# Post-norm transformer block on one core: the inverse softmax sums and the output weights brought into place by DMAs instead of TensorE transposes

## The chip, the cores and the metric

One core of one Trainium2 chip. The metric is the device time of one execution, in microseconds (us). Its engines work side by side, each through its own list of instructions in order: TensorE (PE in the profile), VectorE (DVE), ScalarE (ACT), GpSimd (POOL), and SyncE (SP), which here only issues DMAs. They wait for one another by semaphores. An engine that waits holds up everything behind the wait in its list, DMAs that it was to issue included.

## The reference, cut to what matters

```python
x = L0_attn_x                                   # (4, 512, 512), float32
x = _layernorm(x + attention(x, w_qkv, b_qkv, w_out, b_out))   # 16 heads of 32, causal softmax
x = _layernorm(x + ffn(x))                      # silu(x Wg^T) * (x Wu^T), then Wd^T; 512 -> 2048 -> 512
# attention: scores = q k^T / sqrt(32) + causal; attn = softmax(scores); out = (attn v) @ w_out.T + b_out
# Wg, Wu, Wd = (int32 weight - 128) * scale per row
```

## The kernel before, in words

Every product in float32 precision is made of two halves, `hi` (rounded, float32r) and `lo` (the rest), so a projection is three matmuls for each of four chunks of the contraction (12 for a tile of 128 x 512).

**Attention** is worked off in 16 **groups** (`GROUPS`): group G = 4b + g has the four heads g of batch b. Each group has 16 **steps** (`STEPS`), and every engine's list is written by the same double loop over groups and steps. In a group:

- step 0 begins on TensorE with the products of probabilities and values that the group before has left (`weighted_values`, L1397), then come scores of query block 2 (step 0), of block 3 (step 3), and of blocks 0 and 1 of the *next* group (step 8). DVE takes each row's maximum from PSUM (`tile_max`, L1054) and ACT the exponentials with their row sums (`exponential`, L846).
- `transpose_task` (L1376) turns the probabilities on TensorE in ten tasks at steps 0, 3, 8, 10, 12 and 15; ACT (even ones, L898) and DVE (odd ones, L497) copy them to `probsT`.
- between them TensorE does **filling** matmuls from a list (`filling`, with how many at each step): values (`v`, L1315), queries and keys (`q`, `k`, L1297) of groups to come, output projections (`o`, L1334) of the batch before. When such a tile is complete, DVE takes it at the next step: for `o` with `outputs` (L1092) and `output_statistics` (L1070, L1072) at the end of the step.
- the output of the group's heads is gathered in `pv_acc`. `inverse_sum` (L1061) makes 1/sum for each query, which lies along partitions, but is wanted along the free dimension. POOL widens it to 32 copies for each head (`widen_inverse`, L729), TensorE transposes that at step 15 (`transpose_inverse`, L1408, four transposes), ACT keeps it in `attT` (`keep_inverse`, L854). In the next group DVE multiplies at step 1 (`normalise`, L1067), ACT rounds at step 2 (`att_hi`, L860), POOL subtracts (`att_lo`, L697). The first products of step 8 wait for `normed`, since they write `pv_acc` again.

Three PSUM banks (`WORK`) go round among filling tiles, transposing tasks, weight tiles and inverse transposes; the order in which they are used (`Banks`) is worked out ahead, and each use waits until the bank's former content is drained.

The 16 weight tiles are transposed on TensorE (`transpose_weights`, L1263), rounded by ACT (`w_hi`, L827) and subtracted by DVE (`w_lo`, L1020). The four of `w_out` come at steps 5 and 13 of groups 3 and 4.

**The next batch's input** comes transposed by DMAs: `turn` (L552) issues 8 transposing DMAs of 16-bit halves, `store_halves` (L556) writes them to DRAM, `load_halves` (L560) reads them back so that POOL can `join` (L718) the halves. From `turn(4)` on the same path brings the first layer norm's output for the feed-forward part.

**SyncE's list** in group G, in this order: load for the scan (a check of the feed-forward weights by ACT, steps 6 and 14; the load waits until the buffer's former content is scanned); `load_halves` in g = 0; `turn` in g = 2; in g = 3 the stores of y1 and the next residual (in the last batch: `load_short(0)`), then `store_halves`. After the groups: scales (L625 to L627), `load_halves(5)`, `load_short(1)`, (2), (3). `load_short(r)` (L580, L583, L586) issues 12 transposing DMAs with a quarter of the gate, up and down weights: 4 each.

**Feed-forward**, batch 0: TensorE does 16 matmuls of gate and up (L1508, L1509) for each of 16 hidden tiles and, one tile later, 8 of down (L1515, L1516). ACT widens the staged weights just ahead (`widen_piece`, L918, L923), makes `silu` (L948) and the product's `hi`; DVE the product and its `lo`. ACT's first silu waits for all three scales:

```python
act.wait_ge(scales_loaded, 48)
...
for i in range(NI):
    gate_out(0, i, gate_acc[first_bank(i)])
```

Of the kernel before, what the change touches and what calls it, by code (L numbers as in the profile page):

```python
# [6 lines left out]
def postln_block_kernel(nc: bass.Bass, x, w_qkv, b_qkv, w_out, b_out, gate_w, gate_scale, up_w, up_scale,  # L7
# [13 lines left out]
    P = 128  # L21
# [32 lines left out]
    def scores_at(G, s):  # L54
        if G == GROUPS - 1:
            return {0: (0, (3,))}.get(s)
        if G == GROUPS - 2 and s == 13:
            return 1, (2,)
        return SCORE_STEPS.get(s)

    def maxima_at(G, s):
        if G == GROUPS - 1:
            return {0: (0, 3, (0, 1)), 1: (0, 3, (2, 3))}.get(s)
        if G == GROUPS - 2 and s == 13:
            return 1, 2, (0, 1, 2, 3)
        return MAX_STEPS.get(s)

    def exponentials_at(G, s):
        if G == GROUPS - 1:
            return {1: (0, 3, (0, 1)), 2: (0, 3, (2, 3))}.get(s)  # L70
        if G == GROUPS - 2 and s > 13:
            return 1, 2, ((0, 1), (2, 3))[s - 14]
# [4 lines left out]
    def tasks_of(hf):  # L77
# [9 lines left out]
    INVERSE_STEP = 15  # L87
    SLOTS = 7
    X_STEPS = [1, 2, 3, 4]
    X_FIRST = [3, 5, 6, 7]  # L90
# [3 lines left out]
        (kind, n) for n in range(2, NG) for kind in "qk"] + [("o", n) for n in range(ND)]  # L94
    NW = len(W_TILES)
    W_STEPS = {(0, 4): 8, (0, 7): 9, (1, 4): 10, (1, 7): 11, (3, 5): 12, (3, 13): 13, (4, 5): 14, (4, 13): 15}
# [7 lines left out]

    W_PLACES = NW - ND

    def w_place(i):
        return i if i < W_PLACES else w_tile("v", i - W_PLACES)

    def w_row(i):  # L110
        kind, n = W_TILES[i]
        return "qkvo".index(kind) * D + n * P
# [9 lines left out]
    def filling(G):  # L122
# [15 lines left out]
        return (before + ahead, AMONG_X) if b < LAST else (before, [4, 4, 0, 4, 0, 4, 2, 0, 2, 0, 2, 0, 2, 0, 0, 0])  # L138
# [59 lines left out]
    for G, (jobs, counts) in enumerate(FILLING):  # L198
        for s in range(STEPS):
# [8 lines left out]
            if s == INVERSE_STEP:  # L208
                banks.whole(("r", G))
# [14 lines left out]
    halves_dram = [None] + [nc.dram_tensor(f"halves{n}", (2 * D, S), U16, kind="Internal").ap() for n in range(1, 2 * B)]  # L224
    x_v = x.rearrange("b (t p) d -> b p t d", p=P)
# [36 lines left out]
    LEVEL_FRONT, LEVEL_INVERSE, LEVEL_PROBS = 40, 16, 24  # L262
# [10 lines left out]
    with ctx:  # L273
# [30 lines left out]
        w_stage = sb("w_stage", [P, W_PLACES, D], F32, front)  # L304
# [13 lines left out]
        wT_hi = sb("wT_hi", [P, ND, NE + D], F32R, att)  # L318
        wT_lo = sb("wT_lo", [P, ND, NE + D], F32R, att)
# [3 lines left out]
        inv_sum = sb("inv_sum", [P, NT, HG], F32, att)  # L323
        sb("level_inverse", [P, LEVEL_INVERSE], F32, att)
        inv_wide = sb("inv_wide", [P, NT, HG, HD], F32, att)
# [71 lines left out]
        xT_done = sem("xT_done")  # L397
        z_loaded = sem("z_loaded")
# [8 lines left out]
        inv_widened = sem("inv_widened")  # L407
# [90 lines left out]

        def y_whole(b):
            return z_tok if isinstance(b, int) and b == 0 else yT_next  # L500
# [8 lines left out]

        block = ctx.enter_context(nc.Block())  # L510

        @block.sync
        def _(sp):

            def load_w(i):
                kind, n = W_TILES[i]
                src = w_out[n * P:(n + 1) * P, :] if kind == "o" else w_qkv[w_row(i):w_row(i) + P, :]
                if i >= W_PLACES:
                    wait_drained(sp, "w", w_place(i))
                sp.dma_start(w_stage[:, w_place(i), :], src).then_inc(w_loaded[i], 16)  # L520
# [15 lines left out]
            for i in range(8, W_PLACES):  # L536
# [24 lines left out]

            def store_y1(b):
# [28 lines left out]
            for i in range(W_PLACES, NW):  # L591
                load_w(i)
# [4 lines left out]
            for G in range(GROUPS):  # L597
                b, g = divmod(G, NG)
                if G in SCAN_GROUPS[1:]:
# [7 lines left out]
                if g == 2:  # L607
                    turn(b + 2)
# [9 lines left out]
                if g == 3:  # L618
                    store_halves(b + 2)

# [46 lines left out]
        def _(pool):  # L667
# [58 lines left out]
            def widen_inverse(G):  # L726

                wait_alone(pool, inv_done, 2 * (G + 1))
                nc.gpsimd.tensor_copy(inv_wide[:, :, :, :], inv_sum[:, :, :].unsqueeze(3).broadcast_to(  # L729
                    (P, NT, HG, HD))).then_inc(inv_widened, 1)  # L730

            def add_bias(b):
# [3 lines left out]
                for t in range(NT):  # L736
                    last = nc.gpsimd.tensor_tensor(residual(b)[:, t, :], residual(b)[:, t, :], bias_o[:, :], ALU.add)  # L737
                last.then_inc(res_ready, 1)
# [24 lines left out]
            for G in range(GROUPS):  # L763
                b, g = divmod(G, NG)
                if g == 2:
                    join(b + 1)
                    if b > 0:
                        next_lo(b + 1, 0)
                        next_lo(b + 1, 1)
                if G > 0:  # L770
                    att_lo(G - 1)
                if g == 2 and b > 0:
                    next_lo(b + 1, 2)
                    next_lo(b + 1, 3)
                if G == GROUPS - 1:
                    apply_norm(LAST - 1, 2)
                    apply_norm(LAST - 1, 3)
                    store_third()
                    choose_path()
                widen_inverse(G)  # L780
                if 1 <= G <= 3 * CHUNKS:
                    shorten(G - 1)
                if g == 2 and b > 0:
                    for t in range(NT if b < LAST else 2):
# [3 lines left out]
            add_bias(LAST)  # L788
# [31 lines left out]
        def _(act):  # L820
# [21 lines left out]

            def exponential(G, qb, j):
# [4 lines left out]

            def keep_inverse(G):
                wait_full(act, "r", G)  # L850
                if G > 0:

                    act.wait_ge(att_ready, G)
                nc.scalar.activation(attT[:, :], bank_of("r", G)[:, :], ACT.Copy).then_inc(drained_of("r", G), 1)  # L854
# [32 lines left out]
            for G in range(GROUPS):  # L887
                b, g = divmod(G, NG)
                for s in range(STEPS):
                    for c in x_at(G, s):  # L890
                        next_hi(b + 1, c)
                    if exponentials_at(G, s):
# [6 lines left out]
                    if s == 2 and G > 0:  # L899
# [3 lines left out]
                    if s == INVERSE_STEP:  # L903
                        keep_inverse(G)
# [739 lines left out]
```

## Time and profile before

| | |
|---|---|
| median of 3 runs | 739.49 us (738.57, 739.49, 745.54) |
| the profiled execution | 738.95 us, span 737.0 us, mean granted TensorE clock 0.993 |
| TensorE matmul busy | 713.1 us (97%) |
| TensorE weight load busy | 552.3 us (75%) |
| DVE / ACT / POOL busy | 390.2 (53%) / 373.7 (51%) / 182.1 us (25%) |
| DMA | 83.35 MB, 113 GB/s on the mean |

The span is from the first to the last instruction; the execution's own time is 1.9 us longer. Busy shares are over the whole span; the attention part ends at about 379 us, and the feed-forward part takes the rest.

### The profile page before, as it was taken

The page shows a single profiled execution, that of the slowest core. Times are in us where ns is not written, and L with a number is a line of the kernel's source. Part 1 is how long each engine was busy: PE and PEld are TensorE (multiplying, and loading weights), DVE is VectorE, ACT ScalarE, POOL GpSimd, SP SyncE. Part 2 cuts the span into 40 slices and gives each one's busy share as a digit, 9 for nine tenths or more (in the row PEclk, how much of TensorE's full clock was granted, in tenths as well). Part 3 has the DMA queues.
Part 4 walks back from the last instruction along what each step waited for, and adds up shares of the span by engine and source line. Part 5 has one row for each costly group of instructions (what it writes and reads, how often), then busy time and mean ns, then how long its engine had stood idle before and what let it go on. Part 6 is the DMA issues. An engine that isn't in the chain of part 4 may idle for free.

```text
span 737.0 us, 11734 instructions
## 1 busy us (share of the span) xinstructions
PE 713.1 (97%) x4368; PEld 552.3 (75%) x4368; DVE 390.2 (53%) x992; ACT 373.7 (51%) x900; POOL 182.1 (25%) x194
## 2 busy tenths in 40 slices
PE   7999899999999999999899999999999999999994
PEld 5776676677777777776578888888888888888883
DVE  4766766566666666677543232453334532544336
ACT  3676676667866776777656555322232222322230
POOL 0011310437122660416655242221020001000004
PEclk9999999999999999999999999999999999999998
DMA  9811553336741567314498964872331003000111
GB/s 305 231 66 29 80 146 119 86 95 119 219 144 58 117 171 223 81 41 115 106 217 162 199 161 143 183 217 85 136 66 57 0 35 136 0 1 1 57 58 59
DMA packets 97207, 83.35 MB, mean 113 GB/s; under 512 B 64128, under 2 KB 73344, under 8 KB 97024
## 3 DMA queue, kind: packets, MB, share of 16 engines
q1 hardware_dynamic: 90624, 62.69, 30.6%
q0 software_dynamic: 6528, 19.93, 12.7%
q8 instruction: 34, 0.56, 0.3%
q14 instruction: 21, 0.17, 0.1%
HBM read 59.53 MB, written 22.02 MB: 111 GB/s over the span
## 4 chain that ended last, share of the span: by engine, by line
PE 90%; POOL 3%; ACT 2%; DVE 2%; DMA 1%; issue 0%; SPq 0%; POOLq 0%; DVEq 0%
PE bank L1508 16%; PE bank L1509 16%; PE bank L1297 12%; PE bank L1376 9%; PE bank L1516 7%; PE bank L1515 7%; PE bank L1315 6%; PE bank L1359 6%; PE bank L1397 5%; PE bank L1334 4%; ACT probs L846 1%; DVE probs L1054 1%; PE bank L1408 1%; PE bank L1263 1%; DMA x_tok<-in_L_attn_x_dram 1%; POOL scan_buf L737 1%
## 5 line engine op out<-in xcount | busy, mean ns | idle before, releaser
L846 ACT ACTIVATE probs<-probs,neg_max 128x128 f32<-128x128 f32 (+3 forms) x256 | 140.4, 552 | 3.9 <-DVE neg_max L1054 3.9
L1054 DVE CUSTOM_DVE_ANT_0 probs<-bank,causal 128x128 f32<-128x128 f32 (+3 forms) x256 | 111.7, 484 | 40.2 <-PE bank L1359 40.0
L1170 DVE SCALAR_TENSOR_TENSOR hid<-bank,u_scale,silu 128x512 f32<-128x512 f32 x64 | 48.1, 751 | 157.5 <-PE bank L1509 156.3
L1508 PE MATMUL bank<-xT_hi,gateT 128*128 128x512 f32 x256 | 99.7, 389 | 0.0
L1509 PE MATMUL bank<-xT_lo,gateT 128*128 128x512 f32 x256 | 99.6, 389 | 0.0
L1508 PE MATMUL bank<-xT_hi,upT 128*128 128x512 f32 x256 | 99.6, 389 | 0.0
L1509 PE MATMUL bank<-xT_lo,upT 128*128 128x512 f32 x256 | 99.6, 389 | 0.0
L1376 PEld LDWEIGHTS bank<-ident,probs 128*128 128x128 f32 x640 | 72.1, 142 | 34.0 <-issue 24.7
L948 ACT ACTIVATE silu<-bank,g_scale 128x512 f32<-128x512 f32 x64 | 44.0, 687 | 102.2 <-PE bank L1509 102.2
L898 ACT ACTIVATE probsT<-bank 128x512 f32<-128x512 f32 x80 | 47.7, 596 | 94.9 <-PE bank L1376 93.2
L954 ACT ACTIVATE hid_hi<-hid 128x512 fp32r<-128x512 f32 x58 | 36.7, 632 | 108.6 <-DVE hid L1170 108.6
L1515 PE MATMUL bank<-downT,hid_hi 128*128 128x512 f32 x232 | 90.2, 389 | 0.0
L1516 PE MATMUL bank<-downT,hid_lo 128*128 128x512 f32 x232 | 90.2, 389 | 0.0
L1376 PE MATMUL bank<-ident,probs 128*128 128x128 f32 x640 | 89.2, 279 | 1.0 <-ACT probs L846 0.5
L497 DVE COPY probsT<-bank 128x512 f32<-128x512 f32 x80 | 54.9, 686 | 26.3 <-PE bank L1376 26.3
L1174 DVE TENSOR_TENSOR hid_lo<-hid,hid_hi 128x512 fp32r<-128x512 f32 x58 | 41.5, 715 | 40.5 <-ACT hid_hi L954 40.5
L1508 PEld LDWEIGHTS bank<-xT_hi,gateT 128*128 128x128 f32 x256 | 48.0, 188 | 10.3 <-DVE hid L1170 0.4
L1509 PEld LDWEIGHTS bank<-xT_lo,upT 128*128 128x128 f32 x256 | 48.1, 188 | 10.0
L1509 PEld LDWEIGHTS bank<-xT_lo,gateT 128*128 128x128 f32 x256 | 48.1, 188 | 10.0
L1508 PEld LDWEIGHTS bank<-xT_hi,upT 128*128 128x128 f32 x256 | 48.0, 188 | 10.0
L1297 PE MATMUL bank<-xT_hi,wT_hi 128*128 128x512 f32 x128 | 54.9, 437 | 0.2
L1359 PE MATMUL bank<-k_sb,q_sb 32*128 32x512 f32 (+3 forms) x512 | 48.1, 467 | 2.6 <-DVE neg_max L1054 2.5
(106 smaller groups left out, 1159.9 us busy)
## 6 DMA issues: line engine op xcount, KB each, us to landing
halves<-x_tok SPq DMA_DIRECT2D x7, 1024.0 KB, 6.2
x_tok<-halves SPq DMA_DIRECT2D x7, 1024.0 KB, 7.9
scan_buf<-in_L_ffn_gate_w_dram SPq DMA_DIRECT2D x4, 1024.0 KB, 6.0
scan_buf<-in_L_ffn_up_w_dram SPq DMA_DIRECT2D x4, 1024.0 KB, 5.5
scan_buf<-in_L_ffn_down_w_dram SPq DMA_DIRECT2D x4, 1024.0 KB, 5.5
w_int<-in_L_ffn_gate_w_dram POOLq DMA_DIRECT2D x16, 256.0 KB, 3.7
w_int<-in_L_ffn_up_w_dram POOLq DMA_DIRECT2D x16, 256.0 KB, 3.2
w_int<-in_L_ffn_down_w_dram POOLq DMA_DIRECT2D x16, 256.0 KB, 3.8
```

The costliest lines, as they stand in the source:

```text
L497: copy(probsT[:, (G * BLOCKS + i) % SLOTS, :], bank_of("t", G, i)[:, :]).then_inc(drained_of("t", G, i), 1)
L846: nc.scalar.activation(probs[qb][:, j, :], probs[qb][:, j, :], ACT.Exp, bias=neg_max[:, qb, j:j + 1], scale=-1.0, accum_out=row_sum[:, qb, ...
L898: evict_task(act, G, i, lambda o, i: nc.scalar.activation(o, i, ACT.Copy))
L1054: nc.vector.tensor_tensor_reduce(out=probs[qb][:, j, :], in0=score[j][:, first:first + w], in1=causal[:, S - w:S], scale=-SCALE, scalar=-F ...
L1170: nc.vector.scalar_tensor_tensor(out=hid[:, i % 2, :], in0=bank[:, :], scalar=u_scale[:, i:i + 1], in1=silu[:, i % 2, :], op0=ALU.mult, op ...
L1297: last = nc.tensor.matmul(acc[:, :], w[:, c, e], xT[:, c, :], start=at == 0, stop=at == MM - 1)
L1359: last = nc.tensor.matmul(score[j][:, first:first + w], q_sb[G % 2][rows, qb * P:(qb + 1) * P], k_sb[G % 2][rows, 0:w], start=True, stop=True)
L1376: last = nc.tensor.transpose(acc[:, m * P:(m + 1) * P], probs[qb][:, j, kb * P:(kb + 1) * P], ident[:, :])
L1508: nc.tensor.matmul(acc[n][:, :], w[:, c, cols], form(xT_hi[:, c, :]), start=c == 0, stop=False)
L1509: last = nc.tensor.matmul(acc[n][:, :], w[:, c, cols], form(xT_lo[:, c, :]), start=False, stop=c == ND - 1)
L1515: nc.tensor.matmul(down_acc[t][:, :], form(hi[:, tok]), w_down[:, i, :], start=i == 0, stop=False)
L1516: return nc.tensor.matmul(down_acc[t][:, :], form(lo[:, tok]), w_down[:, i, :], start=False, stop=i == NI - 1)
```

## The change

- The output weights are no longer transposed on TensorE. SyncE issues 8 transposing DMAs of 16-bit halves in group 0 (`turn_w`), stores them to DRAM and loads them back in group 1; POOL joins them in group 3 (`join_w`), ACT rounds them in group 4 at steps 3, 5, 7, 9 (`w_out_hi`), POOL subtracts (`w_out_lo`).
- The inverse sums: DVE writes them with another layout, transposes them in blocks of 32 x 32 at step 8 (`turn_inverse`), a DMA stores them to DRAM (16 KB) and a second one loads them back, repeated over 32 partitions for each head, into `inv_rows`. SyncE issues both, with a wait for the first ahead of the second; for the last group ACT does, at steps 8 and 10. POOL's widening, the four transposes and ACT's copy go.
- `normalise` moves from step 1 to step 5, `att_hi` from step 2 to step 6; in the last group both stand in step 0.
- `inverse_sum` of the second half moves from step 9 to step 8 (step 5 in the last group).
- In g = 2 SyncE does the inverse's store and load, then the scan load of the following group, and then `turn`.
- POOL instead of DVE subtracts for batch 1 (`next_lo`); the last batch's bias is added in two halves earlier; all four `apply_norm` of batch 2 come in group 14.
- Scores, maxima and exponentials of the last group's query block 2 move from steps 13 to 15 of group 14 into step 0 of group 15; the filling of group 14 ends at step 6.

```diff
     PRODUCT_STEPS = [8, 8, STEPS, STEPS, STEPS, STEPS]
-    INVERSE_STEP = 15
+    TURN = 32
+    STORE_STEP, SPREAD_STEP = 8, 10
-    X_FIRST = [3, 5, 6, 7]
+    X_FIRST = [3, 4, 5, 6]
-    W_STEPS = {(0, 4): 8, (0, 7): 9, (1, 4): 10, (1, 7): 11, (3, 5): 12, (3, 13): 13, (4, 5): 14, (4, 13): 15}
+    W_STEPS = {(0, 4): 8, (0, 7): 9, (1, 4): 10, (1, 7): 11}
+    W_OUT_STEPS = [3, 5, 7, 9]
-        return (before + ahead, AMONG_X) if b < LAST else (before, [4, 4, 0, 4, 0, 4, 2, 0, 2, 0, 2, 0, 2, 0, 0, 0])
+        return (before + ahead, AMONG_X) if b < LAST else (before, AMONG_X[:8] + [0] * (STEPS - 8))
+        def store_inverse(eng, G):
+            eng.wait_ge(inv_turned_done, G + 1)
+            eng.dma_start(inv_dram.rearrange("j (q a r) -> (j q) a r", a=P // TURN, r=TURN).rearrange("c a r -> a c r"),
+                          inv_turned[:, :]).then_inc(inv_stored, 16)
+        def load_inverse(eng, G):
+            eng.wait_ge(inv_stored, 16 * (G + 1))
+            if G > 0:
+                eng.wait_ge(normed, G)
+            eng.dma_start(inv_rows[:, :], inv_dram[:, 0:S].unsqueeze(1).broadcast_to((HG, HD, S))).then_inc(inv_spread, 16)
...
 # SyncE
+            def spread_inverse(G):
+                store_inverse(sp, G)
+                load_inverse(sp, G)
             for G in range(GROUPS):
                 b, g = divmod(G, NG)
-                if G in SCAN_GROUPS[1:]:
+                if G in SCAN_GROUPS[1:] and g != 3:
                     load_scan(SCAN_GROUPS.index(G))
...
                 if g == 2:
+                    spread_inverse(G)
+                    if G + 1 in SCAN_GROUPS:
+                        load_scan(SCAN_GROUPS.index(G + 1))
                     turn(b + 2)
...
                 if g == 3:
                     store_halves(b + 2)
+                if g != 2 and G < GROUPS - 1:
+                    spread_inverse(G)
+                if G == 0:
+                    turn_w()
+                if G == 1:
+                    store_w()
+                    load_w_halves()
...
 # POOL
+                    if b == LAST:
+                        add_bias(LAST, range(QH))
                 if G == GROUPS - 1:
-                    apply_norm(LAST - 1, 2)
-                    apply_norm(LAST - 1, 3)
+                    add_bias(LAST, range(QH, NT))
                     store_third()
                     choose_path()
-                widen_inverse(G)
+                if G == NG - 1:
+                    join_w()
+                if G == NG:
+                    for c in range(ND):
+                        w_out_lo(c)
...
-            add_bias(LAST)
 # ACT
-                    if s == 2 and G > 0:
+                    if s == 6 and 0 < G < GROUPS - 1:
                         att_hi(G - 1)
-                    if s == INVERSE_STEP:
-                        keep_inverse(G)
+                    if s == STORE_STEP and G == GROUPS - 1:
+                        store_inverse(act, G)
+                    if s == SPREAD_STEP and G == GROUPS - 1:
+                        load_inverse(act, G)
 # DVE
+            def turn_inverse(G):
+                if G > 0:
+                    dve.wait_ge(inv_stored, 16 * G)
+                wait_alone(dve, inv_done, 2 * (G + 1))
+                nc.vector.transpose(inv_turned[:, :], inv_sum[:, :, :].rearrange("p j q -> p (j q)")).then_inc(inv_turned_done, 1)
             def normalise(G):
-                wait_drained(dve, "r", G)
+                dve.wait_ge(inv_spread, 16 * (G + 1))
+                if G > 0:
+                    dve.wait_ge(att_ready, G)
                 dve.wait_ge(pv_full, G + 1)
-                nc.vector.tensor_tensor(attT[:, :], pv_acc[:, :], attT[:, :], ALU.mult).then_inc(normed, 1)
+                nc.vector.tensor_tensor(attT[:, :], pv_acc[:, :], inv_rows[:, :], ALU.mult).then_inc(normed, 1)
-                    if s == 1 and G > 0:
+                    if s == 5 and 0 < G < GROUPS - 1:
                         normalise(G - 1)
-                    if s == 9:
+                    if s == (8 if G < GROUPS - 1 else 5):
                         inverse_sum(G, 1)
+                        turn_inverse(G)
 # TensorE
-                    if s == INVERSE_STEP:
-                        last_products = products_at(STEPS) if G == GROUPS - 1 else []
-                        for m in last_products[:-1]:
-                            weighted_values(G, m)
-                        transpose_inverse(G)
-                        for m in last_products[-1:]:
+                    if s == STEPS - 1 and G == GROUPS - 1:
+                        for m in products_at(STEPS):
                             weighted_values(G, m)
```

## Rows read from the trace of the kernel before

**Rows 1.** The page's chain that ended last: share of the span by engine.
```profile
PE 90%; POOL 3%; ACT 2%; DVE 2%; DMA 1%; issue 0%; SPq 0%; POOLq 0%; DVEq 0%
```
**Rows 2.** The chain in order of time: start us, us, what. Starts of groups.
```profile
89.80 1.65 PE bank L1397 x32
...
137.56 1.65 PE bank L1397 x32
...
159.35 1.65 PE bank L1397 x32
...
331.82 0.44 PE bank L1408 x4
...
333.63 1.65 PE bank L1397 x32
```
**Rows 3.** Timeline of SyncE's queue: start us, us, line, operation, tiles, count.
```profile
180.02 0.37 SPq L571 DMA_DIRECT2D scan_buf<-in_L_ffn_down_w_dram  x1
...
338.26 10.26 SPq L552 DMA_TRANSPOSE x_tok<-y_scratch  x8
350.22 5.53 SPq L580 DMA_TRANSPOSE stage<-gate_short  x4
...
361.01 5.17 SPq L586 DMA_TRANSPOSE stage<-down_short  x4
...
372.80 2.90 SPq L627 DMA_DIRECT2D d_scale<-in_L_ffn_down_scale_dram  x1
...
387.57 5.17 SPq L586 DMA_TRANSPOSE stage<-down_short  x4
```
**Rows 4.** Waits, whole span: who waited for whom, us in total, times, longest.
```profile
PE bank L1408 <- DVE wT_lo L1020: 2.0, 2, 1.0
```
**Rows 5.** Timeline of DVE and TensorE in group 5.
```profile
142.61 0.68 DVE L1067 TENSOR_TENSOR attT<-bank,attT 128x512 f32<-128x512 f32 x1
...
148.18 0.18 DVE L1072 BATCH_NORM_AGGREGATE ln_mv<-ln_stat 128x2 f32<-128x6 f32 x1
...
148.18 0.86 PE L1397 MATMUL bank<-probsT,v_tok 128*32 128x256 f32 x16
```
**Rows 6.** The chain in order of time, group 2.
```profile
74.83 1.64 DVE xT_lo L1033
...
77.69 0.14 issue
```
**Rows 7.** Timeline of DVE and TensorE in group 8.
```profile
212.17 0.69 DVE L1054 CUSTOM_DVE_ANT_0 probs<-bank,causal 128x512 f32<-128x512 f32 x1
...
213.58 0.86 PE L1397 MATMUL bank<-probsT,v_tok 128*32 128x256 f32 x16
```
**Rows 8.** DMA issues, whole span: tiles, count, KB each, median us to landing.
```profile
out_dram<-z_tok SPq DMA_DIRECT2D x16, 256.0 KB, 2.0
...
y_scratch<-z_tok SPq DMA_DIRECT2D x12, 256.0 KB, 5.6
...
d_scale<-in_L_ffn_down_scale_dram SPq DMA_DIRECT2D x1, 256.0 KB, 6.3
```
**Rows 9.** DMA issues from 176 to 206 us (issued at 189.72).
```profile
halves<-x_tok SPq DMA_DIRECT2D x1, 1024.0 KB, 8.8
```
**Rows 10.** Timeline of DVE in group 14.
```profile
345.50 0.69 DVE L497 COPY probsT<-bank 128x512 f32<-128x512 f32 x1
```
**Rows 11.** Timeline of ACT at the start of the feed-forward part.
```profile
381.05 0.69 ACT L948 ACTIVATE silu<-bank,g_scale 128x512 f32<-128x512 f32 x1 [0.54 <-PE bank L1509]
...
394.42 1.32 ACT L918 ACTIVATE downT<-stage,minus_zero 128x512 fp32r<-128x512 bf16 x2
```
**Rows 12.** The chain in order of time: gate matmuls of hidden tile 4.
```profile
399.08 0.23 PE bank L1508
```
**Rows 13.** Windows: stretch, its length, busy TensorE (instructions), granted clock, DMA share, GB/s.
```profile
80.00:82.00 2.00, 2.00 (x8) 0.50 0.54 123
```
**Rows 14.** The chain in order of time, end of the last group.
```profile
374.79 1.25 POOL attT_lo L697
```

More of the change, by code:

```diff
@@ L515, in load_w @@
             def load_w(i):
[L516 to L520, printed above, removed]
+                sp.dma_start(w_stage[:, i, :], w_qkv[w_row(i):w_row(i) + P, :]).then_inc(w_loaded[i], 16)
             def load_x(t):
@@ L560, in load_halves, with turn_w, store_w, load_w_halves @@
                 sp.dma_start(halves_short, halves_dram[n].rearrange("(c p h) s -> p c (h s)", p=P, h=2)).then_inc(halves_loaded, 16)
+            def turn_w():
+                for t in range(NT):
+                    wait_full(sp, "w", w_tile("v", t))
+                for e in range(2 * ND):
+                    sp.dma_start(w_place.rearrange("p c (e s) -> p (c e) s", e=2)[:, e, :],
+                                 w_out.bitcast(U16)[:, e * P:(e + 1) * P], transpose=True).then_inc(w_turned, 16)
+            def store_w():
+                sp.wait_ge(w_turned, 16 * 2 * ND)
+                sp.dma_start(w_halves_dram.rearrange("(e p) s -> p e s", p=P),
+                             w_place.rearrange("p c (e s) -> p (c e) s", e=2)).then_inc(w_halves_stored, 16)
+            def load_w_halves():
+                sp.wait_ge(w_halves_stored, 16)
+                sp.dma_start(w_place, w_halves_dram.rearrange("(c p h) s -> p c (h s)", p=P, h=2)).then_inc(w_halves_loaded, 16)
             def store_y1(b):
@@ L783, in _ @@
                 if g == 2 and b > 0:
-                    for t in range(NT if b < LAST else 2):
+                    for t in range(NT):
                         apply_norm(b - 1, t)
@@ L891, in _ @@
                         next_hi(b + 1, c)
+                    if s == 0 and G == GROUPS - 1:
+                        exponential(G, 2, 0)
+                        exponential(G, 2, 1)
+                        att_hi(G - 1)
+                        exponential(G, 2, 2)
+                        exponential(G, 2, 3)
                     if exponentials_at(G, s):
@@ L1136, in _ @@
                         take(job)
+                    if s == 0 and G == GROUPS - 1:
+                        for j in range(HG):
+                            tile_max(G, 2, j)
+                        normalise(G - 1)
                     if maxima_at(G, s):
@@ L1156, in _ @@
                             output_statistics(*job[1:])
-                    if g == 2 and s == (13 if b == LAST else 9) and b > 0:
+                    if g == 2 and s == 9 and b > 0:
                         variance(b - 1, mv_done, var_done)
@@ L1262, in transpose_weights @@
                 for c in range(ND):
-                    last = nc.tensor.transpose(acc[:, c * P:(c + 1) * P], w_stage[:, w_place(i), c * P:(c + 1) * P], ident[:, :])
+                    last = nc.tensor.transpose(acc[:, c * P:(c + 1) * P], w_stage[:, i, c * P:(c + 1) * P], ident[:, :])
                 last.then_inc(full_of("w", i), 1)
@@ L1437, in _ @@
                 for s in range(STEPS):
+                    if s == 0 and G == GROUPS - 1:
+                        scores(G, (2,))
                     for m in products_at(STEPS) if s == 0 and G > 0 else ():
```

102 lines of the change are left out of this document (48 added, 54 removed).

## The prediction

> **What bounds the kernel now.** I read the page's chain first: it is TensorE for nine tenths [rows 1], so a microsecond taken from its stream before the feed-forward part is a microsecond of the kernel, unless another wait takes its place. I then followed the chain in order of time. Groups 5 to 13 each take 21.8 us (137.56 to 159.35), almost without a gap; groups 3 and 4 take 23.9 each (89.80 to 137.56, halved) [rows 2]. Group 14 starts at 333.63 (call it T). After 379 us the feed-forward matmuls run without a gap up to the last tail, so what counts there is when they start and whether their weights and scales are staged. That hangs on SyncE's queue, which from 338 us on issues transposing DMAs back to back [rows 3].
>
> **Removed from TensorE.** Four transposes of the inverse cost the chain 0.44 us a group [rows 2]. Before group 14 there are 14 groups: 6.2 us. The output weights' four tiles made groups 3 and 4 longer by 2.1 us each, 4.2 together: two times 0.44 of transposes a group, the rest waits on the rotating banks (the inverse's transposes waited 2.0 us for wT_lo) [rows 4]. Both go: 10.4 us. A tile's two instructions on ACT and DVE, ACT's keep of the inverse and POOL's widening were beside TensorE and count nothing; without the keep and the widening the last group's end loses a link, below.
> The Trainium skill (VectorE: DVE Perf Modes, The three transpose paths) gives 390 ns for a 128x128 transpose on TensorE, in bf16. By it the 80 removed ones would be worth 31 us; the row says 0.11 each, since they follow one another closely, and the sum goes by the row.
>
> **Added on DVE.** `normalise` moves from step 1 to step 5, and TensorE's first products at step 8 wait for it. In group 5 it ran at 142.61, when DVE had time; at its new place it stands behind the statistics of the output tile, the last of which starts at 148.18, the very moment at which TensorE's products start [rows 5]. So normalise runs at about 148.29 to 148.97 (0.68), and the products follow 0.14 later, as scores follow DVE elsewhere [rows 6]: 149.1, a stall of 0.94 us. Groups 5, 6, 9, 10, 13 and 14 have such output tiles: 5 x 0.94 = 4.7 before group 14, the sixth inside it. Where the fill is values (group 8), the maxima end at 212.86 and TensorE comes at 213.58 [rows 7]: normalise ends 213.46, so 0.05 a group, 0.3 for six. DVE's block transpose has no row; it takes between 0.18 and 0.69 us (the shortest and the usual DVE operation of these rows [rows 5, 7]); I take 0.3, hidden except in group 1, where TensorE already waits for DVE: 0.3.
> In group 2 four x_lo subtractions leave DVE, one of which stood in the chain with 1.64 us [rows 6]. But the products now wait there for normalise behind the same maxima, so I count 0.2 gained, not 1.6. POOL does them after its join; queries need them at steps 8 and 10, when they are barely done. ACT's four weight evictions in group 4: 0.2. All other POOL work (join of w_out, its subtractions, the bias) is hidden by POOL's waiting; if that cover went, group 5's first output tile would wait.
>
> **SyncE, groups 7 and 11.** SyncE waits in its queue for the inverse of group 6 (10), then for the scan at step 14, issued at 180.02 before, and only then issues the 8 transposes, which took 10.26 alone at 338.26 [rows 3]. I take 12.5 beside the scan load. They end some 12 us into group 7; y1's four stores land 5.6 after issue [rows 8], some 6.5 in all; z_tok's and the halves' 2 MB go out at +19, and the halves land 8.8 after issue [rows 9], at +28. The inverse of group 7 is queued behind them, so its store lands at about +28.5, which is 7 us into group 8; its spreading load lands between 2.0 (quiet) and 6.3 us later (the other load that repeats rows) [rows 8], so at +9.3 to +13.5; normalise wants it at +9.9. The next scan load goes out behind it and comes late for ACT as well. I take 1.2 us for each of groups 8 and 12, 2.4; ends 0 and 8.
> The Trainium skill (DMA: Bandwidth & Descriptors, Queues, rings and completion order) says that a ring's descriptors start in order, by which the small store waits for both megabytes. If it were let past them, these 2.4 us would be zero. No row here shows a small DMA behind a large one.
>
> So group 14 starts 6.2 + 4.2 + 0.2 - 4.7 - 0.3 - 0.5 - 2.4 = 2.7 us earlier, at T' = T - 2.7.
>
> **SyncE, groups 14 and 15: the decisive step.** Before, SyncE issued the next batch's 8 transposes (10.26) at 338.26, waited for the last output tile, and began the first feed-forward chunk at 350.22 = T+16.6; a chunk is 12 transposing DMAs, 16.0 us [rows 3]. Now the store and load of group 14's inverse stand ahead of the 8 transposes, and the store waits for step 8 on DVE. There DVE's eviction started at 345.50 [rows 10]; six more matmuls at step 6 (6 x 0.23), the stall of 0.94 and the output tile's work now ahead of it move it by 2.0, and reciprocal and transpose end at T'+15.2. Store 0.05 + 2.0 to landing (the quietest DMA row [rows 8]), load issue 0.5, transposes 10.3: the chunk starts at T'+28.3 instead of T+16.6, 11.7 us later. Everything behind it in this queue moves along: scales (d_scale issued at 372.80, landed 6.3 later [rows 3, 8]), load of halves, second chunk.
> How much cover is there? The second chunk's down weights are issued by 392.74 and ACT used them at 394.42 without waiting [rows 3, 11], so they had landed within 1.7. Now they land by T'+72.5. ACT widens two (1.3), does silu (0.7), DVE the product (0.75), and the gate matmuls of hidden tile 4 start at T'+75.3. Before they started at 399.08 = T+65.5 [rows 12]. That is 9.8 later. On the way, scales landing at T'+57.2 hold back the first silu, which started at 381.05 = T+47.4 [rows 11]; that costs the first 8 of the 9.8. Chunks 3 and 4 follow after 16 to 17 us each, while TensorE takes 21.8 for one (4 tiles of 24 matmuls at 0.227), so from there the slack grows and the matmuls are again back to back.
> TensorE stands idle for about 8 us there. In the one such place before, after group 2's scores had waited for the maxima until 77.8, the granted clock stood at 0.50 from 80 to 82 [rows 13], which loses 1 us. Here the wait of 1.8 at tile 4 takes the same up: counted nothing.
> The last group itself: POOL no longer has four bias additions ahead of the last att_lo at 374.79 [rows 14]. Yet the softmax of its block 2 moves into it, att_lo of group 14 stands behind four apply_norms, and the inverse's two DMAs (ACT's queue) end the group. I get the same T'+45.5 for the first gate matmul; up to 3 us less is possible. With SyncE 8 us later than that, either changes nothing.
>
> **Sum.** -2.7 + 9.8 = +7.1 on the profiled execution's 738.95 (span 737.0 and 1.9 around it): 746.0. The runs' median, 739.49, is 0.5 above that execution; against it this is +0.9%. What a measurement can tell from no change is about 1%, here below 732.1 or above 746.9.
>
> **Rivals.**
> 1. As summed, 742 to 750: 0.52. The ends are group 8 and 12 without stall and small costs at zero (-4), or with three more us (+4).
> 2. The spreads of groups 7 and 11 come late in full: 4 us at groups 8 and 12, with ACT's scan behind them. 738.95 + 7.1 + 5.6 = 751.7: 0.14. For it: both megabytes in one queue. Against: the load may be quick.
> 3. SyncE's delay is covered (the transposes issue faster, or the feed-forward start waits for something else anyway): 738.95 - 2.7, less up to 3 at the end of the last group: 733 to 736: 0.10. Against it: scales had only 2 us in hand.
> 4. Normalise at step 5 doesn't stall TensorE and groups 8 and 12 don't either: 7.4 less, 738.6, no change: 0.10. Against it: DVE's order is fixed and the two times coincide to 0.01 us.
> 5. Both 3 and 4: 738.95 - 10.1 - 0 to 3 = 726 to 729. This is the faster case: it is decided at the chunk's start; if that is by T'+19 the gain of TensorE stays. 0.10.
> 6. The removed TensorE work buys nothing, because the bank rotation waits elsewhere: 748 to 753: 0.04.
>
> **Numbers.** Prediction 746.0. Range 735 to 752: it leaves out rival 5, the lower part of 3 and the upper of 2 and 6. Faster: rival 5 and a bit of 3, 0.11. Slower: 0.45 of case 1 (0.23), rival 2, rival 6: 0.40. Within 1%: 0.49.
>
> **What would show it.** Right: no inverse transposes; groups 3 and 4 near 21.4; groups 5, 6, 9, 10 about 0.5 us longer than before, TensorE waiting for attT at step 8; SyncE's first transposes of gate_short some 28 us after group 14's start; ACT's first silu waiting for scales or SyncE's issue; TensorE idle about 8 us after the second pair of gate and up tiles. Wrong: gate_short's transposes issued by T'+19, a gapless feed-forward start, or groups of 21.4 us throughout.

## The result and the profile after

The changed kernel takes 744.62 us (median of 20 runs, 741.51 to 757.14), beside 739.7 for the kernel before, measured with it. The ratio is 1.0071, 95% interval [1.005, 1.0091]: slower by 0.7%, inside the 1% that the prediction called no change, and 1.4 us below the forecast of 746.0. The size is right; two of the terms behind it are not. In the quick profile below both came out smaller than forecast, +2.6 us in sum where +7.1 had been counted, and the median lies above that profile. A second set of runs of the same kernel gave 746.6 (742.08 to 756.43), ratio 1.0076 [1.0047, 1.0104]. Medians and ranges here are of all runs, while a ratio leaves out runs more than 1.5% above the quickest of their kernel, of which the late profile is one and the profiles of e2 and e3, with the same waits, are not. The kernel before scatters by 2 to 3 us (one of its 20 runs, 745.54, apart), this one by 15. So two profiled executions are read below: a quick one (741.51, span 739.6, "the quick profile") and a late one (756.43, span 754.5, from the experiment `a1_again`).

The page's chain of the quick profile, as [rows 1]: TensorE lost five points and SyncE's queue, which was nothing, took seven.

```profile
PE 85%; SPq 7%; DVE 4%; DMA 1%; POOL 1%; issue 1%; ACT 0%; POOLq 0%; DVEq 0%
```

The chain in order of time, as [rows 2]: starts of groups 3, 5, 6, 8 and 14.

```profile
88.61 1.65 PE bank L1468 x32
...
131.35 1.65 PE bank L1468 x32
...
153.59 1.65 PE bank L1468 x32
...
197.18 1.65 PE bank L1468 x32
218.56 1.65 PE bank L1468 x32
...
328.30 1.65 PE bank L1468 x32
```

Groups 3 and 4 take 21.37 each (131.35 - 88.61, halved) and not 23.9; group 5 takes 22.24 and not 21.8; group 8 takes 21.38. Group 14 starts at 328.30, which is 5.3 before the old 333.63. From there to the end of the span it is 411.3 us, where it was 737.0 - 333.63 = 403.4: 7.9 are lost behind group 14's start. -5.3 + 7.9 = +2.6, the difference of the two spans.

SyncE's queue, as [rows 3], and ACT's own queue in the last group:

```profile
343.55 0.54 SPq L508 DMA_DIRECT2D inverses<-inv_turned  x1
345.51 0.54 SPq L515 DMA_DIRECT2D inv_rows<-inverses  x1
346.15 10.28 SPq L570 DMA_TRANSPOSE x_tok<-y_scratch  x8
356.52 5.16 SPq L620 DMA_TRANSPOSE stage<-gate_short  x4
...
377.98 1.14 SPq L675 DMA_DIRECT2D d_scale<-in_L_ffn_down_scale_dram  x1
...
391.63 5.18 SPq L626 DMA_TRANSPOSE stage<-down_short  x4
```

The inverse's store goes out at T'+15.25 (T' = 328.30) and gate_short's first transpose at T'+28.2. TensorE in the last group and at hidden tile 4, the waits from the timeline:

```profile
345.60 1.09 PE L1447 MATMUL bank<-ident,probs 128*128 128x128 f32 x8 [1.39 <-DVE probsT L504]
...
357.40 0.59 PE L1405 MATMUL bank<-wT_hi,attT_hi 128*128 128x512 f32 x1 [2.16 <-POOL attT_lo L745]
...
368.99 0.86 PE L1468 MATMUL bank<-probsT,v_tok 128*32 128x256 f32 x16 [2.70 <-ACT probsT L960]
...
375.59 0.50 PE L1405 MATMUL bank<-wT_hi,attT_hi 128*128 128x512 f32 x1 [1.44 <-POOL attT_lo L745]
...
378.44 0.39 PE L1567 MATMUL bank<-xT_hi,gateT 128*128 128x512 f32 x1
...
401.29 0.50 PE L1567 MATMUL bank<-xT_hi,gateT 128*128 128x512 f32 x1 [1.58 <-DVE hid L1242]
```

The first gate matmul starts at T'+50.1, hidden tile 4's at T'+73.0. ACT, which feeds both:

```profile
363.16 1.11 ACTq L508 DMA_DIRECT2D inverses<-inv_turned  x1
...
367.65 0.56 ACTq L515 DMA_DIRECT2D inv_rows<-inverses  x1
368.25 0.60 ACT L960 ACTIVATE probsT<-bank 128x512 f32<-128x512 f32 x1 [3.34 <-DMA inverses<-inv_turned]
...
383.48 0.69 ACT L1014 ACTIVATE silu<-bank,g_scale 128x512 f32<-128x512 f32 x1 [3.50 <-DMA d_scale<-in_L_ffn_down_scale_dram]
...
398.48 1.34 ACT L984 ACTIVATE downT<-stage,minus_zero 128x512 fp32r<-128x512 bf16 x2 [3.34 <-DMA stage<-down_short]
```

Now the late profile. Its chain through groups 7 and 8 (start, us, what) leaves TensorE altogether:

```profile
187.56 1.26 SPq L570
190.45 6.83 DMA y_scratch<-z_tok
198.28 8.57 DMA inverses<-inv_turned
206.88 5.46 DMA inv_rows<-inverses
212.36 0.70 DVE attT L1136
213.11 1.51 PE bank L1468 x16
```

A store of the inverse that lands in 1.94 us when the queues are quiet (343.55 in the quick profile) took 8.57 behind z_tok's and the halves' 2 MB, and the whole load took 5.46. (In the quick profile the same store went out at 194.75 and its load at 200.28, so behind the same 2 MB it took about 5.5 there too, and that was early enough.) Normalise and TensorE's first products waited for it. The groups' lengths, from the first `pv_acc` products of one to those of the next, put most of the difference between the quick and the late profile, 10.5 of 14.9 us, into two groups; 3.0 more lie behind group 14's start and 1.4 ahead of group 1:

```
                    group 5  group 8  group 12  1 to 14   from 14 on   median of runs
before              21.79    21.78    21.78     287.8     403.4        738.4 - 739.7
after, quick        22.24    21.38    21.35     282.8     411.4        744.6
a1_again (late)     22.24    26.82    26.37     293.3     414.4        746.6
e1_turn_first       22.23    31.67    29.23     301.0     409.7        747.6
e2_normalise_step1  21.36    28.60    26.78     291.3     414.8        753.8
e3_last_inv._early  22.22    21.36    28.42     289.8     417.6        751.2
e4_spread_first     22.23    21.38    21.38     282.8     412.4        744.3
e5 (e4 + e1)        22.23    21.36    21.36     282.8     415.7        740.2
e6 (e4 + e1 + e3)   22.24    21.36    21.37     282.8     405.8        737.2
e7 (before + wait)  21.82    21.83    21.79     287.3     413.3        748.1
e8 (e4 + e2)        21.38    23.14    22.51     281.5     411.5        740.7
e9 (all four)       21.38    22.64    22.44     281.0     409.0        736.3
```

Each row is one profiled execution, in us ("1 to 14": from the start of group 1 to that of group 14; "from 14 on": to the span's end); the medians are of all runs.

### The profile page after: what moved, and what is told of

The parts are those of the page before. It is cut to its first block, busy times and chain, and to the rows that moved or that the text cites. A ratio compares the mean times of both kernels' runs of the same rounds, so it can differ in the third digit from the quotient of the medians.

```text
span 739.6 us, 11582 instructions
## 1 busy us (share of the span) xinstructions
PE 706.7 (96%) x4288; PEld 546.2 (74%) x4288; DVE 387.2 (52%) x1001; ACT 365.7 (49%) x884; POOL 185.7 (25%) x190
## 4 chain that ended last, share of the span: by engine, by line
PE 85%; SPq 7%; DVE 4%; DMA 1%; POOL 1%; issue 1%; ACT 0%; POOLq 0%; DVEq 0%
PE bank L1567 15%; PE bank L1568 15%; PE bank L1369 12%; PE bank L1447 9%; PE bank L1575 7%; PE bank L1574 7%; PE bank L1387 6%; PE bank L1430 6%; PE bank L1468 5%; PE bank L1405 2%; DVE probs L1115 2%; SPq L623 2%; SPq L620 2%; SPq L570 1%; SPq L626 1%; PE bank L1335 1%
## 5 line engine op out<-in xcount | busy, mean ns | idle before, releaser
L745 POOL TENSOR_TENSOR attT_lo<-attT,attT_hi 128x512 fp32r<-128x512 f32 x16 | 20.3, 1271 | 208.6 <-ACT attT_hi L916 208.6
```

## The experiments

Two theories. **Q**: SyncE's queue behind group 14's start is what the change pays with. **D**: the spreads of groups 7 and 11 land late, in some executions or in all, and TensorE waits in groups 8 and 12. Each was measured beside the kernel before (738.4 to 738.8); the ratio is to it.

**a1_again**, the changed kernel once more.

> The changed kernel once more, for comparison on one chip and for a second profile. Both theories: median 744 us (ratio to before 1.007), executions spread from 741 to 752 us. Theory D (the spread comes from DMAs landing late in groups 8 and 12): a slower profile shows TensorE waiting for attT at step 8 of group 8 or 12 for 1 us or more. Theory Q (it comes from SyncE's queue at groups 14 and 15): groups 8 and 12 stay at 21.4 us and only the feed-forward start moves.

746.6 (742.08 to 756.43), 1.0076 [1.0047, 1.0104], and the late profile above.

**e1_turn_first**, SyncE's order in group 14:

```diff
-                    spread_inverse(G)
+                    if b < LAST:
+                        spread_inverse(G)
                     ...
                     turn(b + 2)
+                    if b == LAST:
+                        spread_inverse(G)
```

> The changed kernel, but in group 14 SyncE issues turn(5) ahead of the inverse's store and load, so that the first feed-forward chunk can start about 18 us after group 14 instead of 28. Theory Q (SyncE's order sets the end): the chain no longer passes SyncE's transposes, ACT's first silu no longer waits for a DMA, TensorE's waits after the first gate matmul (2.5 us in the profile) go, and the span falls by 2.5 to 3 us, to about 737; the slow executions gain more, so the median falls by 3 to 5 us to about 740. Rival L (the last group's own chain, from group 14 to the first gate matmul, is what lengthened): the first gate matmul stays at 50 us after group 14's start. Both can hold; if the time doesn't move at all, Q is wrong.

747.61 (739.28 to 758.19), 1.0066 [1.0035, 1.0097]. The expected 740 was missed, and the ratio can't be told from that of the changed kernel. D hides what there is: groups 8 and 12 took 31.67 and 29.23 in its profile, and group 14 started at 346.78. Only the quick end of the runs hints at a gain: four of the 12, 739.28 to 740.49, are below every run of the changed kernel (741.51 and more). Windows of TensorE where hidden tile 4 comes (stretch, length, busy with the instructions, granted clock, DMA share, GB/s) show no gap, so Q's stall in the feed-forward part went, but not the last group's: the first gate matmul stood at 51.4 behind group 14's start.

```profile
412.00:422.00 10.00, 10.00 (x46) 1.00 0.77 198
422.00:432.00 10.00, 10.00 (x46) 1.00 1.10 202
```

**e2_normalise_step1**, DVE normalises at step 1 except in groups 8 and 12:

```diff
-                    if s == 5 and 0 < G < GROUPS - 1:
+                    if s == (5 if G in (8, 12) else 1) and 0 < G < GROUPS - 1:
```

> The changed kernel with normalise back at step 1, except in groups 8 and 12, where the row sums may not have arrived. Theory N (step 5 stalls TensorE behind the output statistics): groups 5, 6, 9, 10, 13 fall from 22.2 to 21.4 us each, 4.3 us together, and what hangs on group 14's step 8 comes as much earlier, with 0.8 more inside group 14: the span falls by 4 to 5 us. Rival (TensorE would wait for something else there): under 1 us.

753.76 (745.99 to 759.75), 1.0161 [1.0126, 1.0196]: slower, where 4 to 5 us less, or by the rival under 1 us, was expected. Group 5 did fall to 21.36; groups 8 and 12, whose normalise the edit leaves alone, took 28.60 and 26.78. That is again D, and only the profile shows the gain in group 5; e8 repeats the edit with the spreads issued earlier.

**e3_last_inverse_early**, ACT's store and load in the last group:

```diff
-                    if s == STORE_STEP and G == GROUPS - 1:
+                    if s == 2 and G == GROUPS - 1:
                         store_inverse(act, G)
-                    if s == SPREAD_STEP and G == GROUPS - 1:
+                    if s == 3 and G == GROUPS - 1:
                         load_inverse(act, G)
```

> The changed kernel, but in the last group ACT issues the inverse's store after step 2 and its load after step 3, instead of steps 8 and 10, so that it doesn't wait for the store between two evictions. Theory L (that wait lengthens the last group): ACT's wait of 3.3 us and TensorE's of 2.7 us go and the first gate matmul comes 3 to 4 us earlier. Theory Q (SyncE's queue sets the end anyway): the total still moves by less than 1 us, because the scales and the second chunk land no earlier.

751.18 (746.3 to 756.91), 1.0159 [1.0122, 1.0197]: some 6 us slower than the changed kernel, which neither theory had. Here group 8 was quick and group 12 late. The last group got its time back: the first gate matmul starts at 379.38, which is 44.3 behind group 14's start and not 50.1. And then ACT waited for the scales, and TensorE for ACT. Waits of TensorE behind group 14's start (who for whom, us, times, longest), then ACT's timeline:

```profile
PE bank L1574 <- ACT gateT L989: 8.3, 1, 8.3
```
```profile
391.89 0.69 ACT L1014 ACTIVATE silu<-bank,g_scale 128x512 f32<-128x512 f32 x1 [7.47 <-DMA d_scale<-in_L_ffn_down_scale_dram]
```

This is the stall of about 8 us that the prediction put there. In the changed kernel it stands in the last group instead. Mending the last group alone hands the wait to the feed-forward part, and there it costs more: from group 14's start on it is 417.6 us, where the quick profile has 411.4 and the late one 414.4. Hidden tile 4 started at 412.71, 77.6 behind group 14's start (quick profile: 73.0), when the second chunk's down weights had landed, some 4 us after their issue was through at 405.78, where the quick profile has 1.7. Behind that wait TensorE ran at the lower clock. ACT's timeline, then windows of TensorE (stretch, length, busy with the instructions, granted clock, DMA share, GB/s):

```profile
409.90 1.33 ACT L984 ACTIVATE downT<-stage,minus_zero 128x512 fp32r<-128x512 bf16 x2 [4.03 <-DMA stage<-down_short]
```
```profile
414.00:416.00 2.00, 2.00 (x6) 0.50 0.97 247
416.00:418.00 2.00, 2.00 (x8) 0.71 1.05 212
```

**e4_spread_first**, theory D alone. In groups 7 and 11:

```diff
                         store_y1(b - 1)
+                        spread_inverse(G)
                         sp.wait_ge(y1_stored, b * (16 * NT))
                         sp.dma_start(z_tok[:, :, :], x_v[b]).then_inc(z_loaded, 16)
                 if g == 3:
                     store_halves(b + 2)
-                if g != 2 and G < GROUPS - 1:
+                if (g < 2 or G == 3) and G < GROUPS - 1:
                     spread_inverse(G)
```

> The changed kernel, with one difference: in groups 7 and 11 SyncE issues the inverse store and load right behind the four y1 stores, ahead of its wait for those stores, of the 1 MB z_tok load and of the 1 MB halves store. Theory D (the scatter of the changed kernel and a part of its loss is the spread of groups 7 and 11 landing late, which TensorE waits for in groups 8 and 12): group 14 starts at 328.3 in every execution, groups 7 to 9 and 11 to 13 take no more than in the quick profile of the changed kernel, the median falls from 744.6 - 746.6 to 741.5 and the runs lie within 2 us of it. Theory Q (the loss is SyncE's queue of group 14 alone): the median stays at 744.6 - 746.6 with the same scatter. In both the part behind group 14's start stays at 411 us.

744.29 (742.7 to 746.21, five runs), 1.0085 [1.0072, 1.0098]. The range went from 15 us to 3.5, and group 14 starts at 328.60. The queue and the chain:

```profile
190.46 0.57 SPq L508 DMA_DIRECT2D inverses<-inv_turned  x1
195.18 0.54 SPq L515 DMA_DIRECT2D inv_rows<-inverses  x1
```
```profile
218.82 1.65 PE bank L1469 x32
...
328.60 1.65 PE bank L1469 x32
```

The median did not fall to the 741.5 that I expected; it is that of the changed kernel. So D explains the slow end of its runs, up to 757, and not its median. What is left lies behind group 14's start, 412.4 us in this profile. Only the quickest of the five runs was profiled, so what moves the others up to 746.21 is open.

**e7_before_with_sync_wait**, theory Q alone, in the kernel before:

```diff
                 if g == 2:
+                    if b == LAST:
+                        sp.wait_ge(inv_done, 2 * (G + 1))
                     turn(b + 2)
```

> The kernel before, with one wait added: in group 14 SyncE waits for that group's inverse row sums before it issues the eight transposes of the halves; nothing else of the change is in it. Theory Q, that this order is what the change pays behind group 14's start: SyncE's queue moves by some 9 us, the first down weights' transposes come too late for the feed-forward, and the time rises by 4 to 8 us, to 743 - 747. Rival (SyncE's queue has slack and the loss is of the last group's softmax and spread): within 1 us of 738.8.

748.07 (747.18 to 748.51), 1.0127 [1.0112, 1.0141]: 9.6 us for one wait on SyncE. In this execution group 14 starts at 332.94 and its chunk at T+24.5 instead of T+16.6. SyncE's queue, then ACT's timeline, then windows of TensorE at hidden tile 4:

```profile
346.31 11.01 SPq L552 DMA_TRANSPOSE x_tok<-y_scratch  x8
357.42 5.12 SPq L580 DMA_TRANSPOSE stage<-gate_short  x4
...
392.95 5.18 SPq L586 DMA_TRANSPOSE stage<-down_short  x4
```
```profile
402.72 1.33 ACT L920 ACTIVATE downT<-stage,minus_zero 128x512 fp32r<-128x512 bf16 x2 [5.96 <-DMA stage<-down_short]
```
```profile
402.00:404.00 2.00, 0.00 (x0) 0.97 1.26 219
404.00:406.00 2.00, 0.47 (x1) 0.50 0.99 242
406.00:408.00 2.00, 2.00 (x6) 0.50 1.02 226
408.00:410.00 2.00, 2.00 (x7) 0.50 0.80 188
410.00:412.00 2.00, 2.00 (x9) 0.82 1.16 200
```

TensorE waits 4.2 us and then runs at the lower clock: 6 and 7 matmuls in 2 us, where this view shows 10 or 11 at full clock. From hidden tile 4 to tile 5 it takes 7.99 us instead of 5.44, another 2.5.

**e5_spread_and_turn_first**, e4 and e1's order together.

> As e4_spread_first, and in group 14 SyncE's eight transposes of the halves stand ahead of the inverse's store and load, so that gate_short's first transposes start near T'+18 and not T'+28. Theory Q (SyncE's lateness starves the first two pairs of feed-forward tiles): the 2.5 us of stalls there and the dip of the clock go, the part behind group 14's start falls from 411.3 to 408 or less, the time is 738. Rival (what is late in the last group is ACT's own store and load of group 15's inverse, behind the traffic of the transposes, and stays late whatever SyncE's order is): the feed-forward stalls go but the last group's waits grow by as much, 741.

740.2 (738.53 to 747.65), 1.0025 [1.0014, 1.0036]: 0.6% quicker than e4. With the late spreads away, SyncE's order shows its worth, 4 us, between the theory and its rival. Its profile is of its slowest run (747.65) and shows the rival's case: the waits in the feed-forward part are gone, but TensorE waits longer in the last group, and the first gate matmul comes 57.5 behind group 14's start (50.7 in e4). The longest wait, which was 4.0 in e4:

```profile
PE bank L1472 <- ACT probsT L964: 5.5, 1, 5.5
```

**e6_spread_turn_first_acts_early**, e5 and e3's edit.

> As e5_spread_and_turn_first, and in the last group ACT issues the inverse's store at step 2 and its load at step 3 instead of 8 and 10. Theory (the two costs behind group 14's start are serial: ACT's in-order wait for its own store in the last group, 5 us, and SyncE's queue in the feed-forward, 3 us; either one mended alone only hands the other more to wait for): both go, the part behind group 14's start is that of the kernel before, 403.4, the time is 734. Rival (ACT waits as long at step 3 as at step 10, since the store lands behind the transposes' traffic): 738 to 741.

737.19 (735.73 to 741.11), 0.9989 [0.9976, 1.0001]. The first gate matmul comes 44.1 behind group 14's start, that 5.5 us wait is no more among the waits, and ACT's store and load of the last inverse go out close together:

```profile
358.20 1.11 ACTq L508 DMA_DIRECT2D inverses<-inv_turned  x1
...
360.31 0.56 ACTq L515 DMA_DIRECT2D inv_rows<-inverses  x1
```

The expected 734 was missed: TensorE waits 2.3 for `hid` and ACT 4.1 for the second chunk's down weights, so SyncE's queue is still some 2 us late (hidden tile 4 starts 67.5 behind group 14's start, before 65.5).

**e8_first_normalise_step1**, e4 and e2's edit.

> e4_spread_first, and DVE normalises the group before at step 1 instead of 5, except in groups 8 and 12 (the edit of e2_normalise_step1, now with the spreads of groups 7 and 11 issued early). My step on normalise (at step 5 it makes TensorE wait 0.9 us in groups 5, 6, 9, 10 and 13): those groups fall from 22.2 to 21.4, group 14 starts at 324, the time is 740. Rival (e2 was slower than the changed kernel since early normalising disturbs something itself, DVE's or POOL's order, and not since groups 7 to 9 and 11 to 13 happened to be the late ones there): 744 or more.

740.7 (738.29 to 742.72), 1.0020 [1.0007, 1.0032], where e4 has 1.0085: by the runs the edit is worth 3 to 5 us once the spreads are issued early (its one profile is 2.0 quicker than e4's), so e2's loss was not the edit alone. Its profile shows the step and its limit. Groups 5, 6, 9, 10 and 13 are 0.86, 0.64, 0.86, 0.64 and 1.19 shorter than in e4, 4.2 in sum. But groups 8 and 12 are 1.8 and 1.1 longer: they start 1.3 earlier, while the scan load, now the last of five transfers in SyncE's queue there, does not. ACT's timeline:

```profile
211.15 1.15 ACT L925 ACTIVATE scan_buf<-scan_buf,minus_exact 128x1024 f32<-128x1024 uint32 x1 [3.61 <-DMA scan_buf<-in_L_ffn_gate_w_dram]
```

In e4 ACT waited 0.90 there. Group 14 starts at 327.5 and not at the 324 that I expected, and takes 20.75 where e4 has 19.25. Why e2's runs fell on the late side more often than those of a1_again (746 to 760 against 742 to 756) is not settled.

**e9_all_four**: e6 and e2's edit.

> e6_spread_turn_first_acts_early with the edit of e8_first_normalise_step1 on top: all four edits to the changed kernel. If they are independent: 737.2 less 4, 733, below both kernels. Rival (with group 14 4 us earlier, SyncE's x_tok and y1 work, or the feed-forward's down weights, are as late as before and take it back): 736 to 738.

736.26 (731.47 to 739.75), 0.9956 [0.9928, 0.9983]. It beats both kernels, the one before by 0.4%, which is clear of the noise of these runs but small. The expected 733 was missed; this is the rival's case. It gives back most of what the edit gave in e8: its waits show the feed-forward part starved again, at the start of hidden tile 4, where e6 had waited 2.3.

```profile
PE bank L1571 <- DVE hid L1246: 4.5, 1, 4.5
```

## Why the prediction came out right

**Removed from TensorE: right.** Groups 3 and 4 lost 2.5 each (23.9 to 21.37), forecast 4.2 in sum for the tiles and 0.44 each for the inverse. Group 7, with nothing else changed in it, takes 21.37 (175.81 to 197.18), forecast 21.8 - 0.44. The price from the row (0.11 a transpose) held.

**Normalise at step 5: right.** TensorE waits for it in the groups with output tiles; group 5 in the quick profile:

```profile
142.84 0.86 PE L1468 MATMUL bank<-probsT,v_tok 128*32 128x256 f32 x16 [0.80 <-DVE attT L1136]
```

0.80 and not 0.94, in groups 5, 6, 9 and 10, and 1.15 in group 13: 4.35 where the sum had 4.7, and 4.2 by e8's groups. The value group 7 shows nothing of the 0.05. DVE's block transpose, for which the prediction had no row, takes 0.21 us (`turn_inverse`, 128x32), forecast 0.3. In group 2 the wait for normalise took 2.62, and the group still came out 0.7 shorter (22.92 for 23.65), as the sum had it (0.44 + 0.2).

**Groups 8 and 12: the step that failed.** I took 1.2 us each, with ends of 0 and 8 together. No execution that was profiled has 1.2: they have 0 (quick profile) or 5.4 and 5.0 (late profile), in the other late ones up to 10.3 (e2 and e3 among them: 7.2 and 5.4; 0 and 7.1). The mechanism was rival 2's, the small store behind both megabytes: issued at 198.28, landed 8.57 later, normalise 3.87 us idle. But it happens or not according to when y1's stores land, for which SyncE waits. In the quick profile they were issued by 188.94, z_tok's load went out at 191.75 and the inverse's at 200.28; in the late one they were issued by 190.91 and the loads at 197.30 and 206.88. Why the same stores land within 2.8 us of the last issue or only after 6.4 is not shown. My price also lacked the clock: 3.83 us of waiting is followed by a stretch at the lower level, 1.2 GHz (granted clock 0.50; windows of TensorE in the late profile),

```profile
212.00:214.00 2.00, 0.89 (x12) 0.78 1.02 379
214.00:216.00 2.00, 2.00 (x28) 0.50 1.03 382
```

and so each late group costs 5 and not 4. This term makes 10.5 of the 14.9 us between the two profiles. The trace agrees with the rule of the Trainium skill (DMA: Bandwidth & Descriptors, Queues, rings and completion order) which the prediction weighed, that a ring's descriptors start in order: in the late profile the small store, issued 0.55 us behind the halves' store, landed within 0.2 us of it (206.9 and 206.7).

**SyncE behind group 14: the mechanism right, the size off by 2.3.** The inverse's store at T'+15.25 (forecast 15.2), the chunk at T'+28.2 (28.3; the parts that I listed add up to 28.05). The second chunk's down weights were issued by 396.81 = T'+68.5, not T'+70.8: the scale loads held the queue for 3.49 and 1.14 us, where the same two took 5.29 and 2.90 before, 3.6 less in sum, and the transposes around them took 1.3 more. Hidden tile 4 starts at T'+73.0, not T'+75.3, which is 7.5 later than before and not 9.8. The 7.9 us of the spans agree. e7 shows the same step by itself at 9.6 us, with a shorter delay of the chunk (7.9), but weights that landed later behind their issue (402.72 after 398.13) and 5 us at the low clock, which I had counted as nothing.

**The last group: missed, and the clock with it.** I had the first gate matmul at T'+45.5; it came at T'+50.1. The waits in the last group sum to 2.16 + 2.70 + 1.44 + 1.39 and some smaller ones, and behind the first the granted clock stood at 0.50 from 358 to 360. I wrote that with SyncE 8 us later neither a quicker nor an equal last group changes anything. e3 shows otherwise. Its last group was 5.8 quicker, so its execution is the one that the forecast describes: first gate matmul at T'+44.3, then TensorE idle for 8.3 us behind the second pair of tiles, as the list of signs has it. It cost 14.2 us more behind group 14's start than before (417.6 and 403.4), where I had counted 9.8. Of the difference 2.3 stand at hidden tile 4 (T'+77.6 for T'+75.3): its down weights were issued when I said (by T'+70.7), but took 4 us to be of use and not the 1.7 of the kernel before. Another 1.8 follow at the lower clock, which I had counted as nothing: from tile 4 to tile 5 it is 7.2 us and not 5.4. The changed kernel took most of its waiting earlier, in pieces of 2.7 us and less, and paid 7.9; for the same reason the sign of 8 idle us is the one of the list that came out otherwise. Why that is the cheaper order is not shown beyond this comparison.

**The sum.** Forecast -2.7 + 9.8 = +7.1. Quick execution: -5.3 + 7.9 = +2.6. Late execution: group 14's start 6.6 later and the rest 414.3 instead of 403.4, +17.5. The median of all, +4.9, lies between. That it is near the forecast's +7.1 is in part luck: -2.7 held 2.4 us of stalls which an execution has either not at all or fourfold, and 9.8 was the right mechanism with queue times that came out shorter, while landing times and a clock that it left out can add up to 4 us, as in e3. The stalls of groups 8 and 12 do not explain the median either, since e4, without them in its profile, has the same (744.3); its distance from the quick profile's 741.5 lies behind group 14's start as far as e4's profile goes (412.4 and 411.4), and the rest is open.

## What to carry to other kernels

Before a small transfer whose landing an engine waits for is put on a queue, look at what is ahead of it: moving it in front of two 1 MB transfers left the median where it was and took the scatter from 15 us to 3.5 (in five runs); the next transfer in the queue (e8's scan load) is then the one to look at. A wait placed on a queue's engine is paid by everything that is queued behind it, even 50 us later and in another stage: one wait on SyncE cost 9.6 us of the kernel before. And when two late chains meet in the same stage, mending one can cost (e3, 6 us) or show an unclear gain (e1); test them together.

## What the runs showed of the hardware

Issuing one and the same small load of scales held SyncE's queue for very different times: u_scale 3.49 us in the quick profile, 5.29 in the kernel before, 6.15 in e5 and 6.50 in e9. A 128x512 normalise on DVE with the spread rows took 0.69 us, against 0.68 with the widened matrix before, so reading the spread rows costs DVE nothing more. A 16 KB store landed in 1.94 us on a quiet queue and in 8.57 behind 2 MB. After waits of 3.83 us (late profile), 4.2 (e7) and 8.3 (e3) TensorE's granted clock stood at 0.50 when the matmuls came again; in e7 it was 0.82 from 410 to 412, the matmuls having run without a gap since 405.5. The length of one wait does not decide it: in the quick profile the clock fell to 0.50 behind a wait of 2.16 (358 to 360), and stayed at 1.00 behind one of 2.70 (368 to 370).
